# Line sweeps of a recurrent convolution: a group's four images interleaved position by position in the working line, PSUM and the sum, in place of image after image

## The chip, the cores and the metric

One core of a Trainium2 chip runs the whole program. The metric is device time in microseconds (us), the median over runs. Engines are named as in the profile: PE is TensorE's matmuls, PEld its weight loads, DVE is VectorE, ACT is ScalarE, POOL is GpSimd, SP is SyncE.

## What is computed

Eight images of 128 channels and 64 x 64 pixels pass through four layers, each of which adds its result to its input. The change touches layer 1 alone. There the image, after a group norm, is swept four times. Each step adds to a line of pixels the rectified convolution of the line before it, which has just been made:

```python
def _propagate(x, w, axis, reverse):
    xm = jnp.moveaxis(x, axis, 0)
    if reverse:
        xm = xm[::-1]
    def step(prev, cur):
        new = cur + jax.nn.relu(_conv1d(prev, w))
        return (new, new)
    _, outs = jax.lax.scan(step, xm[0], xm[1:])
...
x = _propagate(x, w_down, 2, False)
x = _propagate(x, w_up, 2, True)
x = _propagate(x, w_right, 3, False)
x = _propagate(x, w_left, 3, True)
```

`_conv1d` has 9 taps along the line and mixes all 128 channels. Sweeps 0 and 1 go over the rows of the image (down, then up), sweeps 2 and 3 over its columns (right, then left). Each has 63 steps, and no step can start before the one before it in the same image is done.

## The kernel before, in words

The function is `layer1`. Channels lie on the 128 partitions. All eight images stay in SBUF in one tile, `X`, as image, row, column; the sweeps work in place. The images form two groups (`NG` = 2) of four (`NI` = 4), and `s` is the group. The two groups take turns, so that TensorE convolves one while VectorE and ScalarE finish the other: 4 sweeps x 63 lines x 2 groups = 504 turns.

`line(d, s, t)` is the view of `X` that holds line t of sweep d for the four images of group s: in sweeps 0 and 1 four rows, so 64 neighbouring words an image; in sweeps 2 and 3 four columns, so 64 words an image that lie 64 words (256 bytes) apart.

TensorE multiplies in float32r, and fp32 accuracy comes from splitting both operands in a rounded part (hi) and a rest (lo). A turn of group s goes:

- ACT, `round_line` (line 225 of the file): hi = line, rounded. DVE, `rest_of_line` (line 290): lo = line - hi. Both write `prop_parts` (`parts[s]`), which holds hi and lo with a zero at either end of each line.
- PE, line 276: 9 matmuls, one a tap, of `w_lo` with hi, of 240 to 256 columns, into the half `ps[s][:, 1]` of the PSUM bank. Then line 281: 9 matmuls of `w_hi` with hi and lo together, of 480 to 512 columns, into both halves. Edge taps are cut to an even number of positions (`INSIDE`). Line 276 waits for hi (`s_hi`), line 281 for lo (`s_lo`), and the last matmul signals `s_conv`.
- DVE, three instructions: line 305 copies half 1 of the bank to `prop_sum`, line 307 adds half 0, and line 309 does line = max(sum, 0) + line in place in `X`. They are followed by the rest of the new line (290), which has to wait for ACT's rounding (225), which waits for 309.

The order is written out by hand, an instruction stream for each engine with semaphores between them; each engine does what it is given in order. On DVE it is 305, 307, 309, 290 of group 0, then of group 1, then the next line:

```python
with dve.Fori(1, H) as t:
    for s in range(NG):
        dve.wait_ge(s_conv[s], t + LINES * d)
        ...
        rest_of_line(d, t, s)
        if s == 0 and d == 3:
            add_first_x1(t - 1)
```

ACT has beside it, in sweep 0 only, the group norm of the next row (line 230). In sweep 3 DVE adds the layer's input to image 0 (line 296, every other turn). POOL makes `w_lo` once a sweep and prepares weights of layer 2. The other layers have their own functions and come before and after, with a barrier of all engines between.

Of the kernel before, what the change touches and what calls it, by code (L numbers as in the profile page):

```python
# [16 lines left out]
F32 = mybir.dt.float32  # L17
F32R = mybir.dt.float32r
U32 = mybir.dt.uint32
ALU = mybir.AluOpType  # L20
# [3 lines left out]
P = 128  # L24
B, H, W = 8, 64, 64
# [107 lines left out]
def layer1(nc, G, outer, x1_dram):  # L133
# [5 lines left out]
    NG, NI, PAD, LINES = 2, G.NI, 1, H - 1  # L139
    HALFWAY = H // 2  # L140
    MID = TAPS // 2
    INSIDE = [(k, max(0, MID - k) // 2 * 2, W - max(0, k - MID) // 2 * 2) for k in (MID, *range(MID), *range(MID + 1, TAPS))]
    with ExitStack() as ctx:
        def sb(name, shape, dt=F32):
            return ctx.enter_context(nc.sbuf_tensor(name, shape, dt))

        def sem(name):
            return ctx.enter_context(nc.semaphore(name))
        weights2 = Layer2Weights(nc, G, outer, ctx)
        raw = sb("prop_raw", [P, TAPS * P])  # L150
        w_hi = sb("prop_w_hi", [P, 2, TAPS * P], F32R)
        w_lo = sb("prop_w_lo", [P, 2, TAPS * P], F32R)
        parts = [sb(f"prop_parts{s}", [P, 2, NI, W + 2 * PAD], F32R) for s in range(NG)]
        hi = [t[:, 0, :, :] for t in parts]
        lo = [t[:, 1, :, :] for t in parts]
        zero = sb("prop_zero", [P, NI, PAD])
        ps = [ctx.enter_context(nc.psum_tensor(f"prop_ps{s}", [P, 2, NI, W], F32)) for s in range(NG)]
        sums = [sb("prop_sum", [P, NI, W])] * NG
        s_zero, s_edge = sem("p_zero"), sem("p_edges_zero")
        s_late = sem("p_second_halves_landed")  # L160
        s_norm = [sem(f"p_S_normed{s}") for s in range(NG)]
# [13 lines left out]
        def line(d, s, t):  # L175

            idx = t if d % 2 == 0 else t * -1 + (H - 1)
            if d < 2:
                return XV[:, NI * s:NI * s + NI, idx, :]
            return XV[:, NI * s:NI * s + NI, :, idx]  # L180

        with nc.Block() as block:
            @block.sync
            def _(sp):
                sp.dma_start(raw[:], G.d[names[0]]).then_inc(s_raw, 16)
                for b in range(NI, B):
                    sp.dma_start(G.X[:, b, 0:HALFWAY * W], x1_dram[:, b * HW:b * HW + HALFWAY * W]).then_inc(G.x_landed[b], 16)
                for b in range(G.KEEP, B):
                    sp.dma_start(G.X[:, b, HALFWAY * W:HW], x1_dram[:, b * HW + HALFWAY * W:(b + 1) * HW]).then_inc(s_late, 16)
                weights2.load(sp)  # L190
                sp.dma_start(first_x1[:].rearrange("p h w -> p (h w)"), x1_dram[:, 0:HW]).then_inc(G.first_x1_landed, 16)
                for d in range(1, 4):
                    sp.wait_ge(s_wlo, d)
                    sp.dma_start(raw[:], G.d[names[d]]).then_inc(s_raw, 16)
# [72 lines left out]
            @block.tensor  # L267
            def _(pe):
                pe.wait_ge(s_edge, 8)
                for d in range(4):  # L270
                    pe.wait_ge(s_wlo, d + 1)
                    with pe.Fori(1, H) as t:
                        for s in range(NG):
                            pe.wait_ge(s_hi[s], t + H * d)
                            for k, a, b in INSIDE:
                                pe.matmul(ps[s][:, 1, :, a:b], w_lo[:, d % 2, k * P:(k + 1) * P],  # L276
                                          hi[s][:, :, PAD + a + k - MID:PAD + b + k - MID],
                                          start=(k == MID), stop=False, skip_group_check=True)
                            pe.wait_ge(s_lo[s], t + H * d)
                            for k, a, b in INSIDE:  # L280
                                mm = pe.matmul(ps[s][:, :, :, a:b], w_hi[:, d % 2, k * P:(k + 1) * P],  # L281
                                               parts[s][:, :, :, PAD + a + k - MID:PAD + b + k - MID],
                                               start=False, stop=(k == TAPS - 1), skip_group_check=True)
                            mm.then_inc(s_conv[s], 1)

            @block.vector
            def _(dve):
                def rest_of_line(d, t, s):
                    dve.wait_ge(s_hi[s], t + (1 + H * d))
                    dve.tensor_tensor(lo[s][:, :, PAD:PAD + W], line(d, s, t), hi[s][:, :, PAD:PAD + W].bitcast(F32),  # L290
                                      ALU.subtract).then_inc(s_lo[s], 1)

                def add_first_x1(t):
                    dve.wait_ge(s_lo[0], t + (1 + H * 3))
                    x = line(3, 0, t)[:, 0, :]
                    dve.tensor_tensor(x, x, first_x1[:, :, t * -1 + (H - 1)], ALU.add).then_inc(s_added, 1)
                for d in range(4):
                    for s in range(NG):
                        rest_of_line(d, 0, s)
                    if d == 3:  # L300
                        dve.wait_ge(G.first_x1_landed, 16)
# [3 lines that stand above are left out]
                            dve.tensor_copy(sums[s][:], ps[s][:, 1, :, :]).then_inc(s_sum[s], 1)  # L305
                            dve.wait_ge(s_sum[s], 2 * t + (2 * LINES * d - 1))
                            dve.tensor_tensor(sums[s][:], ps[s][:, 0, :, :], sums[s][:], ALU.add).then_inc(s_sum[s], 1)
                            dve.wait_ge(s_sum[s], 2 * t + 2 * LINES * d)
                            dve.scalar_tensor_tensor(line(d, s, t), sums[s][:], 0.0, line(d, s, t), ALU.max,  # L309
                                                     ALU.add).then_inc(s_new[s], 1)  # L310
                            rest_of_line(d, t, s)
                            if s == 0 and d == 3:
                                add_first_x1(t - 1)
                for s in range(NG):
                    dve.wait_ge(s_lo[s], 4 * H)
                add_first_x1(H - 1)
                dve.wait_ge(s_added, H)
# [1534 lines left out]
```

## Time and profile before

| | us |
|---|---|
| median of 3 runs | 7821.44 |
| lowest and highest run | 7798.07, 7832.47 |
| the profiled execution | 7801.72 |
| its span, which the rows below divide | 7799.9 |

Busy over the whole span: PE 75%, DVE 68%, POOL 53%, ACT 46%, weight loads 43%. Layer 1's sweeps take from 2141 to 3774 us, a fifth of the span; layer 0 lies before them and layers 2 and 3 behind. The shares of the whole are averages over those layers and tell nothing of the sweeps, so the rows below are taken from inside each sweep.

### The profile page before, as it was taken

The numbers are of one execution on the slowest core, as the hardware profiler recorded it, in microseconds if no ns is written. First come the engines' busy times: TensorE is split into PE (matmuls) and PEld (weight loads), VectorE is DVE, ScalarE is ACT, GpSimd is POOL, SyncE is SP. The second block draws the span as 40 slices with busy tenths as digits, with TensorE's granted clock in tenths as the row PEclk, the third lists the DMA queues.
The fourth block names the chain that finished last, engine by engine and source line by source line (L and its number), as shares of the span: only waits on it lengthen the run. The fifth ranks groups of instructions, "written<-read, shape, count | busy, mean of one in ns | idle before, by whom it ended". The sixth has DMA issues, their size and how long they took to land. (4 is left out here: it accounts for less than half of the span.)

```text
span 7799.9 us, 91527 instructions
## 1 busy us (share of the span) xinstructions
PE 5869.8 (75%) x21659; PEld 3337.9 (43%) x21659; DVE 5308.8 (68%) x12779; ACT 3557.2 (46%) x7357; POOL 4119.9 (53%) x3880
## 2 busy tenths in 40 slices
PE   5999999999899999999865665656656565565432
PEld 2444444444388888888532322323222222232211
DVE  6999999999855556666465666556565665665557
ACT  4878888888755112222233333333333333333333
POOL 4999999999800001000055555556555555565663
PEclk9999999999999999999987777867778777787665
DMA  5544444444410001000166666566665666666667
GB/s 189 180 173 175 171 170 169 172 165 170 165 52 3 3 0 44 0 0 0 50 176 204 178 186 190 163 196 183 189 194 157 205 175 186 191 176 184 178 182 264
DMA packets 325623, 1132.63 MB, mean 145 GB/s; under 512 B 58859, under 2 KB 59901, under 8 KB 283300
## 3 DMA queue, kind: packets, MB, share of 16 engines
q0 software_dynamic: 188224, 629.56, 27.8%
q1 hardware_dynamic: 136948, 498.69, 17.9%
q14 instruction: 367, 3.01, 0.1%
q8 instruction: 84, 1.38, 0.1%
HBM read 997.72 MB, written 130.29 MB: 145 GB/s over the span
## 5 line engine op out<-in xcount | busy, mean ns | idle before, releaser
L1276 POOL DMA_INDIRECT d_ring<-corner_table,d_idx_now x2304 | 2218.9, 963 | 1704.5 <-issue 979.8
L1474 PE MATMUL d_ps_s<-small,d_mix 128*128 128x128 f32 x2304 | 478.7, 344 | 1317.3 <-DVE d_mix L1646 788.2
L980 POOL TENSOR_TENSOR X<-X 128x512 f32<-128x512 f32 x1024 | 1289.9, 1277 | 167.6 <-DVE X L1018 149.8
L1646 DVE SCALAR_TENSOR_TENSOR d_acc<-d_ring,d_w_now,d_mix 128x128 f32<-128x128 f32 x2304 | 661.0, 355 | 726.7 <-ACT d_mix L1322 347.1
L281 PE MATMUL prop_ps<-prop_parts,prop_w_hi 128*128 128x496 f32 (+2 forms) x4536 | 1142.1, 396 | 0.0
L1018 DVE TENSOR_TENSOR_SCAN X<-X,m_pB 128x512 f32<-128x512 f32 x896 | 1133.9, 1271 | 0.0
L874 PE MATMUL m_pY<-X,small 128*128 128x512 f32 x2048 | 1040.5, 605 | 90.8 <-POOL X L980 90.7
L1474 PEld LDWEIGHTS d_ps_s<-small,d_mix 128*128 128x128 f32 x2304 | 318.8, 172 | 1839.6 <-issue 981.1
L1322 ACT ACTIVATE d_mix<-d_ring,d_w_now 128x128 f32<-128x128 f32 x2304 | 732.5, 391 | 797.7 <-DMA d_ring<-corner_table,d_idx_now 724.0
L281 PEld LDWEIGHTS prop_ps<-prop_parts,prop_w_hi 128*128 128x128 f32 x4536 | 818.7, 189 | 162.1
L1406 PE MATMUL d_ps_out<-d_samp,d_dcn_w 128*128 128x512 f32 x1152 | 825.7, 809 | 46.3 <-ACT X L1309 34.0
L225 ACT ACTIVATE prop_parts<-X 128x256 fp32r (+1 forms) x512 | 276.6, 541 | 1178.1 <-DVE X L309 1177.6
L885 PE MATMUL m_pB<-m_bcs,m_pick 128*128 128x512 f32 x1027 | 759.6, 740 | 0.0
L1008 DVE TENSOR_TENSOR m_pB<-m_dtx,m_pB 128x512 f32<-128x512 f32 x1024 | 694.6, 679 | 92.4 <-PE m_pB L885 67.7
L941 ACT ACTIVATE X<-m_dtv,m_A 128x512 f32<-128x512 f32 x1027 | 688.5, 713 | 96.6 <-POOL m_dtv L737 75.0
L1646 DVE SCALAR_TENSOR_TENSOR d_mix<-d_ring,d_w_now,d_acc 128x128 f32<-128x128 f32 x2304 | 647.1, 341 | 86.6 <-remote 52.6
L1646 DVE SCALAR_TENSOR_TENSOR d_acc<-d_ring,d_w_now,d_acc 128x128 f32<-128x128 f32 x2304 | 649.6, 349 | 48.2 <-DVE d_acc L1646 21.5
L276 PE MATMUL prop_ps<-prop_parts,prop_w_lo 128*128 128x248 f32 (+2 forms) x4536 | 636.4, 285 | 20.9 <-ACT prop_parts L225 11.0
L276 PEld LDWEIGHTS prop_ps<-prop_parts,prop_w_lo 128*128 128x128 f32 x4536 | 608.3, 190 | 84.4 <-ACT prop_parts L225 40.1
L874 PEld LDWEIGHTS m_pY<-X,small 128*128 128x128 f32 x2048 | 363.3, 189 | 471.0 <-POOL X L980 281.3
L290 DVE TENSOR_TENSOR prop_parts<-X,prop_parts 128x256 fp32r<-128x256 f32 x512 | 267.5, 523 | 370.5 <-ACT prop_parts L225 370.3
L1371 ACT ACTIVATE d_tT<-l_ps_b 128x512 f32<-128x512 f32 x240 | 142.6, 594 | 709.4 <-remote 506.9
(232 smaller groups left out, 7840.5 us busy)
## 6 DMA issues: line engine op xcount, KB each, us to landing
X<-c_scratch SPq DMA_DIRECT2D x256, 1024.0 KB, 4.9
corner_table<-d_tT SPq DMA_DIRECT2D x248, 256.0 KB
d_ring<-corner_table,d_idx_now POOLq DMA_INDIRECT x2304
X<-in_x SPq DMA_DIRECT2D x8, 2048.0 KB, 15.2
m_res<-in_x SPq DMA_DIRECT2D x64, 256.0 KB, 4.5
x_scratch<-m_res SPq DMA_DIRECT2D x64, 256.0 KB, 2.1
x_scratch<-X SPq DMA_DIRECT2D x8, 2048.0 KB
b_x<-x_scratch POOLq DMA_DIRECT2D x16, 1024.0 KB, 11.7
```

The costliest lines, as they stand in the source:

```text
L276: pe.matmul(ps[s][:, 1, :, a:b], w_lo[:, d % 2, k * P:(k + 1) * P], hi[s][:, :, PAD + a + k - MID:PAD + b + k - MID], start=(k == MID), st ...
L281: mm = pe.matmul(ps[s][:, :, :, a:b], w_hi[:, d % 2, k * P:(k + 1) * P], parts[s][:, :, :, PAD + a + k - MID:PAD + b + k - MID], start=Fal ...
L874: pe.matmul(pY[:], G.ident, hc[:, n % NHC, :], start=False, stop=(n == NS - 1), skip_group_check=True).then_inc(s.sum, 1)
L885: pe.matmul(pB[:, n % NB, :], T.pick[:, n:n + 1].to_broadcast([P, P]), bcs[:, par, :], start=True, stop=True).then_inc(s.B, 1)
L980: pool.tensor_tensor(hc[:, n % NHC, :], h[:, n, :], Cb[:, n, :], ALU.mult).then_inc(s.HC, 1)
L1008: dve.tensor_tensor(pB[:, n % NB, :], dtx[:, c % 2, :], pB[:, n % NB, :], ALU.mult).then_inc(s.U, 1)
L1018: dve.tensor_tensor_scan(h[:, n, :], dA[:, n % NDA, :], pB[:, n % NB, :], T.zero[:, 0:1] if c == 0 else h[:, n, CH - 1:CH], ALU.mult, ALU. ...
L1276: pool.indirect_dma_start(out=ring[:, m % RING, :], out_offset=None, in_=flat, in_offset=bass.IndirectOffsetOnAxis(ap=idx_now[:, c % 2, m: ...
L1322: r0 = act.activation(R[:, k % 3, t, :], ring[:, m % RING, 0:P], ACT.Copy, scale=w_now[:, c % 2, 4 * m:4 * m + 1])
L1406: pe.matmul(ps_out[:], dcn_w[:, k, :], samp[:, k % 3, :], start=(k == 0), stop=(k == TAPS - 1)).then_inc(s_dcn, 1)
L1474: turned = pe.transpose(ps_s[k % 3][:, t, :], R[:, k % 3, t, :], G.ident)
L1646: mixed = dve.scalar_tensor_tensor(R[:, k % 3, t, :] if corner == 3 else acc[:, t, :], ring[:, m % RING, corner * P:(corner + 1) * P], w_n ...
```

## The change

The tiles `prop_parts`, `prop_ps` and `prop_sum` hold the same numbers in another order. They were (half,) image, position; now they are (half,) position, image, so that the four images' values of one position are neighbours. `X` keeps its order. The matmuls and the two DVE instructions that read PSUM go over the tiles in their order. ACT's rounding, DVE's rest and line 309, which also touch `X`, still go image by image, so in `prop_parts` and `prop_sum` they now step four words (16 bytes) from each element to the next.

```diff
@@ -150,12 +150,12 @@
-        parts = [sb(f"prop_parts{s}", [P, 2, NI, W + 2 * PAD], F32R) for s in range(NG)]
-        hi = [t[:, 0, :, :] for t in parts]
-        lo = [t[:, 1, :, :] for t in parts]
+        parts = [sb(f"prop_parts{s}", [P, 2, W + 2 * PAD, NI], F32R) for s in range(NG)]
+        hi = [t[:, 0, :, :].rearrange("p w i -> p i w") for t in parts]
+        lo = [t[:, 1, :, :].rearrange("p w i -> p i w") for t in parts]
         zero = sb("prop_zero", [P, NI, PAD])
-        ps = [ctx.enter_context(nc.psum_tensor(f"prop_ps{s}", [P, 2, NI, W], F32)) for s in range(NG)]
-        sums = [sb("prop_sum", [P, NI, W])] * NG
+        ps = [ctx.enter_context(nc.psum_tensor(f"prop_ps{s}", [P, 2, W, NI], F32)) for s in range(NG)]
+        sums = [sb("prop_sum", [P, W, NI])] * NG
@@ -273,13 +273,13 @@
                             for k, a, b in INSIDE:
-                                pe.matmul(ps[s][:, 1, :, a:b], w_lo[:, d % 2, k * P:(k + 1) * P],
-                                          hi[s][:, :, PAD + a + k - MID:PAD + b + k - MID],
+                                pe.matmul(ps[s][:, 1, a:b, :], w_lo[:, d % 2, k * P:(k + 1) * P],
+                                          parts[s][:, 0, PAD + a + k - MID:PAD + b + k - MID, :],
                                           start=(k == MID), stop=False, skip_group_check=True)
                             pe.wait_ge(s_lo[s], t + H * d)
                             for k, a, b in INSIDE:
-                                mm = pe.matmul(ps[s][:, :, :, a:b], w_hi[:, d % 2, k * P:(k + 1) * P],
-                                               parts[s][:, :, :, PAD + a + k - MID:PAD + b + k - MID],
+                                mm = pe.matmul(ps[s][:, :, a:b, :], w_hi[:, d % 2, k * P:(k + 1) * P],
+                                               parts[s][:, :, PAD + a + k - MID:PAD + b + k - MID, :],
                                                start=False, stop=(k == TAPS - 1), skip_group_check=True)
@@ -306,7 +306,7 @@
-                            dve.scalar_tensor_tensor(line(d, s, t), sums[s][:], 0.0, line(d, s, t), ALU.max,
+                            dve.scalar_tensor_tensor(line(d, s, t), sums[s][:].rearrange("p w i -> p i w"), 0.0, line(d, s, t), ALU.max,
                                                      ALU.add).then_inc(s_new[s], 1)
```

No instruction is added, dropped or moved on any engine; only the shapes on PE differ. On PE, the matmuls of one turn (the loop body of lines 276 and 281; the shape is that of the output):

```order
-L276 MATMUL prop_ps<-prop_parts,prop_w_lo 128x4x60
-L276 MATMUL prop_ps<-prop_parts,prop_w_lo 128x4x62 x2
+L276 MATMUL prop_ps<-prop_parts,prop_w_lo 128x240
+L276 MATMUL prop_ps<-prop_parts,prop_w_lo 128x248 x2
 L276 MATMUL prop_ps<-prop_parts,prop_w_lo 128x256 x2
```

The matmuls of line 281 change from 128x8x60 and 128x8x62 to 128x2x240 and 128x2x248. What was read as one run an image and half (4 runs, or 8) is now one run a half (1, or 2); this holds for the full-length taps as well, whose input had the two zeros between one image and the next.

## Rows read from the trace of the kernel before

**Rows 1.** Busy time by engine in each of the four sweeps, columns in the second line.
```profile
core 0: us, PE busy (x) PEld busy (x) DVE busy (x) ACT busy (x) POOL busy (x), PEclk, DMA share, GB/s
2141.40:2549.40 408.00, 404.90 (x2268) 352.37 (x2268) 214.39 (x502) 222.29 (x627) 2.67 (x1) 0.99 0.08 30
2549.40:2953.40 404.00, 401.88 (x2267) 350.62 (x2268) 214.87 (x506) 54.51 (x129) 2.64 (x1) 1.00 0.01 2
2953.40:3363.60 410.20, 404.38 (x2281) 351.22 (x2280) 280.66 (x512) 87.73 (x132) 33.84 (x53) 1.00 0.08 21
3363.60:3773.60 410.00, 406.77 (x2260) 337.74 (x2259) 279.27 (x567) 83.42 (x126) 0.00 (x0) 1.00 0.00 0
```

**Rows 2.** Timeline, one turn of sweep 1 (start us, us busy, engine).
```profile
2705.76 1.25 PE L276 MATMUL prop_ps<-prop_parts,prop_w_lo 128*128 128x256 f32 x9
2705.96 0.42 DVE L305 COPY prop_sum<-prop_ps 128x256 f32<-128x256 f32 x1 [0.66 <-PE prop_ps L281]
2706.42 0.42 DVE L307 TENSOR_TENSOR prop_sum<-prop_ps,prop_sum 128x256 f32<-128x256 f32 x1
...
2706.84 2.26 PE L281 MATMUL prop_ps<-prop_parts,prop_w_hi 128*128 128x512 f32 x9
2706.99 0.42 DVE L309 SCALAR_TENSOR_TENSOR X<-prop_sum,X 128x256 f32 x1
2707.53 0.42 ACT L225 ACTIVATE prop_parts<-X 128x256 fp32r x1 [2.69 <-DVE X L309]
2707.99 0.43 DVE L290 TENSOR_TENSOR prop_parts<-X,prop_parts 128x256 fp32r<-128x256 f32 x1 [0.57 <-ACT prop_parts L225]
...
2708.94 1.24 PE L276 MATMUL prop_ps<-prop_parts,prop_w_lo 128*128 128x256 f32 x9
```

**Rows 3.** Timeline, one turn of sweep 2.
```profile
3154.75 0.43 DVE L305 COPY prop_sum<-prop_ps 128x256 f32<-128x256 f32 x1
3155.21 0.42 DVE L307 TENSOR_TENSOR prop_sum<-prop_ps,prop_sum 128x256 f32<-128x256 f32 x1
...
3155.79 0.76 DVE L309 SCALAR_TENSOR_TENSOR X<-prop_sum,X 128x256 f32 x1
3156.67 0.67 ACT L225 ACTIVATE prop_parts<-X 128x256 fp32r x1 [2.55 <-DVE X L309]
3157.36 0.62 DVE L290 TENSOR_TENSOR prop_parts<-X,prop_parts 128x256 fp32r<-128x256 f32 x1 [0.82 <-ACT prop_parts L225]
...
3157.94 0.42 DVE L305 COPY prop_sum<-prop_ps 128x256 f32<-128x256 f32 x1
```

**Rows 4.** Groups in 2555 to 2950 us, sweep 1 (busy us, mean ns, idle before).
```profile
L290 DVE TENSOR_TENSOR prop_parts<-X,prop_parts 128x256 fp32r<-128x256 f32 x124 | 52.8, 426 | 73.2 <-ACT prop_parts L225 73.2
L305 DVE COPY prop_sum<-prop_ps 128x256 f32<-128x256 f32 x124 | 52.7, 425 | 89.7 <-PE prop_ps L281 89.7
L309 DVE SCALAR_TENSOR_TENSOR X<-prop_sum,X 128x256 f32 x124 | 52.7, 425 | 19.5 <-DVE prop_sum L307 10.7
L225 ACT ACTIVATE prop_parts<-X 128x256 fp32r x124 | 51.9, 418 | 344.6 <-DVE X L309 344.6
```

**Rows 5.** The same groups in 2955 to 3360 us, sweep 2.
```profile
L309 DVE SCALAR_TENSOR_TENSOR X<-prop_sum,X 128x256 f32 x127 | 96.6, 760 | 17.8
L290 DVE TENSOR_TENSOR prop_parts<-X,prop_parts 128x256 fp32r<-128x256 f32 x128 | 79.2, 619 | 103.1 <-ACT prop_parts L225 102.9
L305 DVE COPY prop_sum<-prop_ps 128x256 f32<-128x256 f32 x126 | 53.5, 424 | 2.0 <-PE prop_ps L281 2.0
L225 ACT ACTIVATE prop_parts<-X 128x256 fp32r x126 | 83.3, 661 | 319.0 <-DVE X L309 319.0
```

**Rows 6.** Line 96 before the sweeps: three short additions with gaps in every operand.
```profile
L96 DVE TENSOR_TENSOR sums<-sums x3: 189/194/225, 2129.9 to 2130.4; 128x64 f32<-128x64 f32 x1, 128x32 f32<-128x32 f32 x1, 128x16 f32<-128x16 f32 x1
```

## The prediction

> **What bounds the kernel now.** The change touches only the line sweeps, so I read those alone and look for what sets the length of one turn. The view of busy time by stretch comes first [rows 1]: the four sweeps take 408, 404, 410 and 410 us, 1632 in all, with the granted TensorE clock at 0.99 to 1.00, the 2.4 GHz level. With 126 turns a sweep (63 lines, 2 groups) a turn takes 3.2 to 3.25 us. PE is busy for 98 to 99% of every sweep, which makes it look like the bound of all four. That has to be tested against the other engines' order.
>
> The timeline of sweep 1 [rows 2] says yes for that sweep. PE starts line 276 at 2705.76 and again at 2708.94, a turn of 3.18 us. DVE waits for PE before its copy (0.66 us in this turn, 89.7 us in the 124 turns counted [rows 4]). PE bounds.
>
> The timeline of sweep 2 [rows 3] says no. The turn is the same, 3.19 us from copy to copy (3154.75 to 3157.94), but DVE no longer waits for PE: 2.0 us in 126 turns [rows 5]. Its four instructions and ACT's rounding between them form a closed loop, each step released by the one before:
> - copy to add 0.46 us, add to line 309 0.58, line 309 to ACT 0.88, ACT to rest 0.69, rest to the next copy 0.58: 3.19 us.
>
> So in sweeps 2 and 3 DVE and ACT bound the turn, with PE level with them. Sweep 3 has the same loop with line 296 beside it (410 us too). What differs from sweep 1 is only the reading and writing of columns of X. The same loop in sweep 1 [rows 2] is 0.46 + 0.57 + 0.54 + 0.46 up to the start of the rest, and 0.42 more until a copy could start (the rest's own 0.426 [rows 4]; in sweep 2 the copy follows the rest a little before its end): 2.45 us. It has 0.74 us of room under PE's 3.19.
>
> **What the change takes from PE.** It shortens no column count, it joins runs. The 9 matmuls of line 276 have 3 x 256 + 4 x 248 + 2 x 240 = 2240 columns, those of line 281 twice as many. At one column a cycle of 2.4 GHz that is 0.93 and 1.87 us. In the timeline [rows 2] the first nine take 1.08 us (2705.76 to 2706.84), the other nine 2.10 (to 2708.94). The excess is 0.15 and 0.23 us, or 16 ns for a matmul of 4 runs and 26 ns for one of 8. If that is a price by run, it is 2.5 ns a run over a fixed 6. With 1 and 2 runs the excess becomes 8.5 and 11 ns, 0.18 us a turn in place of 0.38. PE's turn falls from 3.18 to an estimated 2.98 us. The bounds: 3.18 (the excess goes with the columns, not the runs) and 2.80 (all of it goes). I take 2.98, because twice the runs over twice the columns would have doubled the fixed part as well.
>
> **What it adds to DVE and ACT.** Three instructions now step four words in a tile where they ran through neighbours. The price of a step is in the trace only for columns of X, by sweep 2 against sweep 1 [rows 4, 5], the same instructions with the same 256 elements:
> - line 290, one stepping input: 426 to 619 ns, +0.19 us.
> - line 309, one stepping input and a stepping output: 425 to 760, +0.335. The second stream adds 0.14 to what the first costs.
> - line 225 on ACT, a stepping input: 418 to 661, +0.24.
>
> Those steps are 256 bytes, the new ones 16. The nearest row to that is line 96 [rows 6]: its 64-element form, in groups of four neighbours, takes 225 ns, the 32-element form in pairs 194, the 16-element form with single words 32 bytes apart 189. From 64 to 32 elements 31 ns go, about 1 ns an element; from 32 to 16 only 5, where 16 would be due. So short steps of single words cost too, by some 11 ns on 16 elements, 0.7 ns each, in an instruction with three such streams. On 256 elements that is 0.18. I take the column prices for the first and second stream, since these are the same instructions on the same tiles.
>
> Sweeps 0 and 1, where X is read and written in runs:
> - line 309, one stepping input: +0.19 (bounds 0 and 0.335).
> - line 225, a stepping output: no row has it; between 0.14 (a second stream on DVE) and 0.24 (an input on ACT): +0.19, bounds 0 and 0.335.
> - line 290, a stepping input and a stepping output: +0.335 (bounds 0 and 0.47, which is 0.335 and one more stream).
> - The loop becomes 2.45 + 0.715 = 3.165 us against PE's 2.98: DVE and ACT take over as the bound, and the turn goes from 3.19 to 3.165. 252 turns x -0.025 = **-6 us**. What PE gains is not used here.
>
> Sweeps 2 and 3, where these instructions step already and the loop has no room:
> - line 309 gets its third stream: between 0 and 0.14, +0.10.
> - line 290 gets a second and a third: between 0 and 0.28, +0.20.
> - line 225 gets a stepping output beside the stepping input: between 0 (the two overlap) and 0.24, +0.12.
> - +0.42 us on a loop that is wholly on the path: 252 x 0.42 = **+106 us**. PE's gain is worth nothing here, since PE only stays level today.
>
> The copy and the add (305, 307) keep one run of 256. The eight small writes of the zeros stay as they are, and the starts of the four sweeps, each one pass through the chain of steps, add under 1 us each. In sweep 0 ACT does the next row's norm too (222 us busy in 408 [rows 1]); 0.19 us more a turn leaves it idle for over 1 us a turn. The clock should hold: PE would be busy for some 83% of the turn, and no sweep shows it at another level. Layers 0, 2 and 3 keep their work, so what the sweeps lose is lost whole.
>
> The sum is +100 us: 7802 for the profiled execution becomes 7902. The median of the runs lies 20 us above that execution, so for the median I give **7920 us**, +1.3%.
>
> A rule weighed against this: sweep 2's row for one stepping input is 619 - 426 = 193 ns on 256 elements, 0.75 ns each, and for two streams 1.3 ns each [rows 4, 5]. The Trainium skill (Vector Engine (DVE) Microarchitecture Reference, Measured stream behaviour on trn2) has 1.05 ns an element in runs of at least two words, 1.73 for one source that hops each element, and 1.98 with all three operands hopping: the later streams nearly free. By it line 290 and line 309 would lose only 0.06 us each in sweeps 2 and 3, and the sum would be about +20 us. The trace agrees on the first stream and not on the second; the second rival below is this case, from rows. The same section has 2.5 ns for steps of 24 words, which is the fourth.
>
> **The rivals.**
> 1. The forecast: steps of four words cost about what columns do. Chance **0.45**. Its own range is 7860 to 8000.
> 2. Penalties saturate: the first stepping stream costs 0.19, later ones on the same instruction nothing. For it: each stream may hide behind another's stall. Against: line 309's second stream cost 0.14. Sweeps 0 and 1: 2.45 + 0.19 + 0.19 + 0.14 = 2.97, so PE at 2.98 bounds, -0.20 x 252 = -50. Sweeps 2 and 3: only ACT, +0.12, 252 x 0.12 = +30. Together -20: 7801 for the median. **0.20**, within 0.5%.
> 3. The other side, faster: a step of four words is free and only long steps cost. Then the loop stays at 2.45 us in sweeps 0 and 1, PE's 2.98 decides, and -0.20 x 252 = -50 us; in sweeps 2 and 3 the loop of 3.19 still binds, 0. That is 7771. It decides where the three steps together add under 0.1 us in sweeps 2 and 3 and under 0.5 in sweeps 0 and 1. For it: the steps are a sixteenth of a column's. Against: line 96's short steps cost. **0.13**. The gain cannot be much larger, for half the turns do not wait for PE. The Trainium skill (SBUF — State Buffer, Door 1, the note on cachelines) says that one can stride for free over 4 fp32, and that each access which crosses to a new 16-byte line pays; a step of exactly 16 bytes stands between the two halves of that sentence. No row of this trace has that step.
> 4. Short steps cost more than columns: each instruction pays what line 309's two streams do (0.335), and line 290 0.47. Sweeps 0 and 1: 2.45 + 1.14 = 3.59, +0.40 x 252 = +101. Sweeps 2 and 3: the same 1.14 on top, +287. Together up to 8210; the near end is 8080. **0.09**.
> 5. The change does nothing for PE: the excess goes with the columns. Then sweeps 0 and 1 stay at 3.19, since 3.165 is still under it, and the sum is +106: 7927. It is told from the forecast only on PE's rows. **0.13**.
>
> **How the numbers follow.** Less than about 0.5% (39 us) can't be told from no change here. Faster by more is rival 3, 0.13. Within it is rival 2, 0.20. Slower is the forecast, rivals 4 and 5, 0.67. The range reaches from 7780, which leaves out half of rival 3, to 8090, which leaves out most of rival 4; about 0.14 is outside.
>
> **What would show it.** Right: in sweeps 0 and 1 line 309 near 0.62 us, line 290 near 0.76, line 225 near 0.61; DVE's idle time before line 305 gone there; nine matmuls of line 276 in about 1.01 us and of line 281 in 1.97 when nothing makes them wait, and PE waiting for ACT's rounding in every sweep. In sweeps 2 and 3 line 309 near 0.86, 290 near 0.82, 225 near 0.78, and turns of 3.6 us. The two row sweeps would keep their 404 to 408 us, the two column sweeps would take some 460 each. Wrong: durations of 0.42 us at these lines in sweep 1 (rival 3), or column sweeps that stay near 410 us (rival 2 or 3), or row sweeps above 440 us (rival 4).

## The result, and the profile after

The change made the kernel a little faster, where I had forecast it 1.3% slower.

| | before | after |
|---|---|---|
| first comparison, median us (range) | 7807.15 (7781.91 to 7832.47) | 7746.90 (7727.66 to 7764.90) |
| ratio, 95% interval | | 0.9927 (0.990 to 0.9954) |
| second comparison, another chip (e5) | 6979.42 | 6954.26 |
| ratio | | 0.9966 (0.9954 to 0.9978) |
| third comparison, a third chip (e10) | 7804.80 | 7763.12 |
| ratio | | 0.9943 (0.992 to 0.9966) |

The first and third chip need 830 us more than the second for the same program. Layers 2 and 3 account for it: 4026 us in the profile of before, 3193 to 3195 in the profiles of e5 and e2, whose layers 2 and 3 are the same. So the sweeps are best compared by themselves. Busy time by engine in each sweep of the changed kernel (the columns are named in the first line):

```profile
core 0: us, PE busy (x) PEld busy (x) DVE busy (x) ACT busy (x) POOL busy (x), PEclk, DMA share, GB/s
2141.80:2539.20 397.40, 390.28 (x2268) 346.18 (x2268) 262.89 (x505) 234.61 (x629) 2.68 (x1) 0.99 0.08 31
2539.20:2930.00 390.80, 387.84 (x2269) 344.73 (x2270) 258.47 (x508) 85.16 (x129) 2.66 (x1) 1.00 0.01 2
2930.00:3331.30 401.30, 397.66 (x2269) 333.92 (x2269) 273.02 (x508) 87.27 (x129) 36.16 (x53) 1.00 0.08 22
3331.30:3747.60 416.30, 411.43 (x2268) 335.15 (x2268) 283.57 (x569) 85.38 (x127) 0.00 (x0) 1.00 0.00 0
```

Against [rows 1] the sweeps take 1606 us in place of 1632, 27 less. Measured from the first matmul of one sweep to that of the next, the four went from 402, 405, 405 and 412 us to 389, 391, 401 and 416 (with 8 us ahead of the first for its weights). The row sweeps gain 13 and 14 us; the column sweeps stay, one 4 us shorter and one 4 longer.

Groups of the changed kernel in 2555 to 2900 us, sweep 1 (busy us, mean ns, idle before); the first four are VectorE's and the last ScalarE's:

```profile
L290 DVE TENSOR_TENSOR prop_parts<-X,prop_parts 128x256 fp32r<-128x256 f32 x113 | 71.3, 631 | 93.9 <-ACT prop_parts L225 93.9
L309 DVE SCALAR_TENSOR_TENSOR X<-prop_sum,X 128x256 f32 x112 | 68.7, 613 | 17.6 <-DVE prop_sum L307 9.6
L305 DVE COPY prop_sum<-prop_ps 128x256 f32<-128x256 f32 x113 | 48.0, 425 | 0.0
L307 DVE TENSOR_TENSOR prop_sum<-prop_ps,prop_sum 128x256 f32<-128x256 f32 x113 | 47.9, 424 | 3.9
L225 ACT ACTIVATE prop_parts<-X 128x256 fp32r x113 | 74.5, 659 | 271.6 <-DVE X L309 271.6
```

The same in 2950 to 3310 us, sweep 2:

```profile
L309 DVE SCALAR_TENSOR_TENSOR X<-prop_sum,X 128x256 f32 x114 | 87.0, 763 | 16.0
L290 DVE TENSOR_TENSOR prop_parts<-X,prop_parts 128x256 fp32r<-128x256 f32 x114 | 72.6, 637 | 94.5 <-ACT prop_parts L225 94.5
...
L225 ACT ACTIVATE prop_parts<-X 128x256 fp32r x114 | 76.7, 673 | 283.0 <-DVE X L309 283.0
```

Read beside [rows 4] and [rows 5]: where nothing stepped before, each of the three instructions now costs 0.19 to 0.24 us more (309: 425 to 613 ns, 290: 426 to 631, 225: 418 to 659). Where one operand or more stepped already, the new steps cost 0.003, 0.018 and 0.012 us. VectorE's wait for PE before line 305 in sweep 1 is gone (89.7 us in [rows 4], 0.0 now), so its loop has grown to nearly the length of TensorE's turn.

The timeline of one turn of sweep 1 after the change:

```profile
2602.05 1.19 PE L276 MATMUL prop_ps<-prop_parts,prop_w_lo 128*128 128x256 f32 x9
2602.25 0.42 DVE L305 COPY prop_sum<-prop_ps 128x256 f32<-128x256 f32 x1
2602.71 0.42 DVE L307 TENSOR_TENSOR prop_sum<-prop_ps,prop_sum 128x256 f32<-128x256 f32 x1
...
2603.07 2.19 PE L281 MATMUL prop_ps<-prop_parts,prop_w_hi 128*128 128x512 f32 x9
2603.27 0.61 DVE L309 SCALAR_TENSOR_TENSOR X<-prop_sum,X 128x256 f32 x1
2604.01 0.67 ACT L225 ACTIVATE prop_parts<-X 128x256 fp32r x1 [2.36 <-DVE X L309]
2604.71 0.63 DVE L290 TENSOR_TENSOR prop_parts<-X,prop_parts 128x256 fp32r<-128x256 f32 x1 [0.83 <-ACT prop_parts L225]
...
2605.10 1.20 PE L276 MATMUL prop_ps<-prop_parts,prop_w_lo 128*128 128x256 f32 x9
```

The turn is 3.05 us here from one start of line 276 to the next. As a mean over the middle of sweep 1 it is 3.06, against 3.18 before. (A sweep's length over its 126 turns is more, 3.10 against 3.21, for it holds the sweep's start.) The nine matmuls of line 276 take 1.02 us in place of 1.08, those of line 281 2.03 in place of 2.10; as means of the sweep they lose 0.05 and 0.06 us.

Which of the two bounds a turn shows in how long after TensorE's last matmul the copy of line 305 starts. In the row sweeps it is 0.04 us in nearly every turn, before the change and after it: TensorE bounds. In sweep 2 the matmuls before the copy at 3157.94 of [rows 3] were these:

```profile
3155.64 2.26 PE L281 MATMUL prop_ps<-prop_parts,prop_w_hi 128*128 128x512 f32 x9
```

and in the changed kernel, in the same sweep:

```profile
3101.65 2.19 PE L281 MATMUL prop_ps<-prop_parts,prop_w_hi 128*128 128x512 f32 x9
...
3103.67 0.63 DVE L290 TENSOR_TENSOR prop_parts<-X,prop_parts 128x256 fp32r<-128x256 f32 x1 [0.83 <-ACT prop_parts L225]
...
3104.22 0.42 DVE L305 COPY prop_sum<-prop_ps 128x256 f32<-128x256 f32 x1
```

Before the change TensorE ended at 3157.90 and the copy followed 0.04 us later, as in 117 of the 126 turns of that sweep. After it TensorE ends at 3103.84 and the copy starts 0.38 us later. So TensorE still bounded sweep 2 before the change, and the loop of VectorE and ScalarE bounds it now; the mean turn went from 3.18 to 3.15 us. In sweep 3 the copy came 0.41 us after TensorE already before the change: the loop bounds it in both kernels, with turns of 3.235 and 3.267 us. The 0.032 us more match the three new steps (0.003 + 0.018 + 0.012).

### The profile page after: what moved, and what is told of

It reads as the page before. It is cut to its first block and busy times, and to the rows that moved or that the text cites. A ratio compares the mean times of both kernels' runs of the same rounds, so it can differ in the third digit from the quotient of the medians.

```text
span 7725.9 us, 91527 instructions
## 1 busy us (share of the span) xinstructions
PE 5818.9 (75%) x21659; PEld 3292.0 (43%) x21659; DVE 5401.5 (70%) x12779; ACT 3601.9 (47%) x7357; POOL 4123.7 (53%) x3880
## 5 line engine op out<-in xcount | busy, mean ns | idle before, releaser
L281 PE MATMUL prop_ps<-prop_parts,prop_w_hi 128*128 128x496 f32 (+2 forms) x4536 | 1108.3, 388 | 0.0
L225 ACT ACTIVATE prop_parts<-X 128x256 fp32r (+1 forms) x512 | 340.5, 666 | 1106.8 <-DVE X L309 1105.9
L276 PEld LDWEIGHTS prop_ps<-prop_parts,prop_w_lo 128*128 128x128 f32 x4536 | 581.4, 189 | 113.6 <-ACT prop_parts L225 87.4
L290 DVE TENSOR_TENSOR prop_parts<-X,prop_parts 128x256 fp32r<-128x256 f32 x512 | 324.5, 634 | 434.0 <-ACT prop_parts L225 434.0
```

Source lines behind the costliest of these rows:

```text
L276: pe.matmul(ps[s][:, 1, a:b, :], w_lo[:, d % 2, k * P:(k + 1) * P], parts[s][:, 0, PAD + a + k - MID:PAD + b + k - MID, :], start=(k == MI ...
L281: mm = pe.matmul(ps[s][:, :, a:b, :], w_hi[:, d % 2, k * P:(k + 1) * P], parts[s][:, :, PAD + a + k - MID:PAD + b + k - MID, :], start=Fal ...
```

## The experiments

### e1: single instructions, each form by itself

Behind the last layer of the kernel before, one block with each form in a loop; the rest of the program is as before. Below, `four` is a tile of 256 words read or written with a step of four, `run` one without a step, `col` a column of `X`, four images.

```diff
+                for _r in range(8):
+                    dve.tensor_tensor(four(2), run(0), four(1), ALU.add).then_inc(s_op, 1)
...
+                for _r in range(24):
+                    last = pe.matmul(q_ps[:, 0:512].rearrange("p (n l) -> p n l", n=8), w32[:], rows(m32, 8, 2), start=True, stop=True, skip_group_check=True)
```

> The kernel before, with a block of single instructions behind its last layer, each form repeated 8 times (VectorE, ScalarE) or 24 times (TensorE). VectorE, 256 fp32 elements, 0.43 us with no stepping operand. Theory A (a step costs once: what counts is whether any operand steps from element to element, not how many): one, two or three stepping operands of four words all take 0.61 to 0.64 us, a column of X as input the same, and only reading and writing the same column in place takes 0.76. Theory B (each stream adds its price): two stepping operands 0.76 or more wherever they lie, three 0.85 or more. ScalarE: 0.42 without, 0.66 with a step on either side, and on both 0.67 (A) or 0.9 (B). TensorE, 512 float32r columns back to back: theory R (a price by run): 1 run 219 ns start to start, 2 runs 221, 8 runs 231 to 240, 32 runs over 270; theory C (a price by column): 231 to 240 in all of them.

Single instructions on VectorE (min/median/max ns). The nine, from the top: no step; one input `four`; output `four`; input and output `four`; all three `four`; one input a column; a column read and written; the same with a `four` input as well (line 309 in the column sweeps); one input with a step of two words.

```profile
L1928 DVE TENSOR_TENSOR X<-X x8: 425/426/426, 6968.3 to 6971.5; 128x256 f32<-128x256 f32 x8
L1932 DVE TENSOR_TENSOR X<-X x8: 604/605/607, 6971.9 to 6976.4; 128x256 f32<-128x256 f32 x8
L1940 DVE TENSOR_TENSOR X<-X x8: 609/610/610, 6982.2 to 6986.7; 128x256 f32<-128x256 f32 x8
L1944 DVE TENSOR_TENSOR X<-X x8: 616/618/623, 6987.4 to 6991.9; 128x256 f32<-128x256 f32 x8
L1948 DVE TENSOR_TENSOR X<-X x8: 608/609/615, 6992.6 to 6997.1; 128x256 f32<-128x256 f32 x8
L1952 DVE TENSOR_TENSOR X<-X x8: 583/586/590, 6997.7 to 7002.1; 128x256 f32<-128x256 f32 x8
L1968 DVE TENSOR_TENSOR X<-X x8: 699/699/700, 7018.8 to 7023.9; 128x256 f32<-128x256 f32 x8
L2000 DVE SCALAR_TENSOR_TENSOR X<-X x8: 719/722/723, 7060.5 to 7065.8; 128x256 f32<-128x256 f32 x8
L2004 DVE TENSOR_TENSOR X<-X x8: 425/426/427, 7066.6 to 7069.8; 128x256 f32<-128x256 f32 x8
```

ScalarE: no step; input `four`; output `four`; a column as input and a `four` output; an input with a step of two words.

```profile
L1844 ACT ACTIVATE X<-X x8: 416/416/417, 7116.8 to 7119.9; 128x256 f32<-128x256 f32 x8
L1848 ACT ACTIVATE X<-X x8: 652/653/654, 7120.4 to 7125.2; 128x256 f32<-128x256 f32 x8
L1852 ACT ACTIVATE X<-X x8: 651/652/652, 7125.9 to 7130.6; 128x256 f32<-128x256 f32 x8
L1864 ACT ACTIVATE X<-X x8: 656/657/657, 7141.9 to 7146.7; 128x256 f32<-128x256 f32 x8
L1868 ACT ACTIVATE X<-X x8: 428/428/428, 7147.4 to 7150.6; 128x256 f32<-128x256 f32 x8
```

Theory A holds for steps of four words. One such stream costs 0.18 us on VectorE and 0.24 on ScalarE, and two or three cost no more than one (0.61 to 0.62 us in all on VectorE, 0.66 on ScalarE). Theory B is right only for a column read and a column written in one instruction: 0.70. It does not take the same column: with one column read and another written it was 0.70 too. In the sweeps line 309 took 0.76 where its form here takes 0.70 to 0.72; why is not shown. On VectorE two words cost nothing, three words 0.07 us (494 ns, line 2008), four words the whole price.

TensorE, 24 matmuls of 512 float32r columns each, in 8, 32 and 64 runs:

```profile
L1896 PE MATMUL q_ps<-q_m,q_w x24: 395/395/400, 7199.5 to 7204.8; 128*128 128x512 f32 x24
L1900 PE MATMUL q_ps<-q_m,q_w x24: 419/420/420, 7210.9 to 7216.8; 128*128 128x512 f32 x24
L1902 PE MATMUL q_ps<-q_m,q_w x24: 447/447/450, 7217.0 to 7223.5; 128*128 128x512 f32 x24
```

Neither R nor C. As a mean from one start to the next it is 234 ns in 8 runs, 257 in 32 and 282 in 64 (a row's duration is 161 to 165 more, for a matmul overlaps the next); 1, 2 and 4 runs are at 233 to 234 as well. At 256 columns it was 114 for 1 run, 120 for 4 and 124 for 8. So breaks cost, but at 512 columns 8 runs took no more than one. Only the input is broken in these rows, the output is one run. The same 512 columns in bf16 took 216 ns, in 1 run or in 32.

### e2 and e3: the copy on ScalarE, before and after the change

Line 305 moves from VectorE to ScalarE, in both kernels alike, which should make the loop of VectorE and ScalarE 0.46 us shorter, so that TensorE's own turn shows in every sweep.

```diff
+                def copy_half(d, t, s):
+                    act.wait_ge(s_conv[s], t + LINES * d)
+                    act.activation(sums[s][:], ps[s][:, 1, :, :], ACT.Copy).then_inc(s_sum[s], 1)
...
-                            dve.wait_ge(s_conv[s], t + LINES * d)
-                            dve.tensor_copy(sums[s][:], ps[s][:, 1, :, :]).then_inc(s_sum[s], 1)
```

> The kernel before with the copy of line 305 moved from VectorE to ScalarE. The loop of VectorE and ScalarE falls by 0.46 us a turn, so TensorE bounds all four sweeps. If TensorE's turn is 3.19 us in the old order of the images: the sweeps take 402, 402, 404 and 404 us, the layer some 1622 us against 1632 (total -10 us, no difference that can be measured). If what follows layer 1 takes longer or shorter by tens of us in a profile although nothing in it has changed, that is scatter of those layers.

> The changed kernel with the same copy on ScalarE. TensorE alone bounds: the turn shows its price in the new order. With the 3.05 us seen in the sweeps of the changed kernel: every sweep 385 to 389 us, the layer some 1555 us, -50 us against the changed kernel and -78 against the one before (total 7720 to 7740 if the later layers stay at 4026 us, 7680 if they stay at the 3978 of the changed kernel's profile). If the loop were still the bound (rival), 390, 391, 401, 416 as in the changed kernel.

e2: 6964.65 us against 6971.89, ratio 0.9993 (0.9984 to 1.0002). Its sweeps take 402, 405, 404 and 406 us. e3: 6917.07 us, ratio 0.9922 (0.9908 to 0.9936). Its sweeps:

```profile
2140.50:2539.00 398.50, 391.22 (x2269) 346.92 (x2269) 211.09 (x379) 298.24 (x755) 2.67 (x1) 0.99 0.08 31
2539.00:2929.60 390.60, 387.77 (x2268) 344.34 (x2268) 210.22 (x381) 133.24 (x255) 2.64 (x1) 1.00 0.01 2
2929.60:3320.50 390.90, 387.70 (x2268) 344.57 (x2268) 231.57 (x381) 135.75 (x256) 35.58 (x53) 1.00 0.08 22
3320.50:3711.60 391.10, 387.82 (x2268) 344.44 (x2268) 243.52 (x444) 134.18 (x254) 0.00 (x0) 0.99 0.00 0
```

The four (the first less its 8 us) lie within 4 us of each other in e2 and within 1 in e3, so TensorE alone bounds there. As means over the middle of a sweep its turn is 3.18 us in the old order and 3.06 in the new, so the new order saves 0.12 us a turn, 14 us a sweep, where TensorE bounds. e3's sweeps came out at 390 to 391 us where I had expected 385 to 389, and the layer at 1571 us for 1555, since 3.05 us a turn leaves out the start of each sweep. In the changed kernel the row sweeps were at that bound already; e3 brings the column sweeps down to it, 10 and 25 us. e3 beats both kernels.

e2 says something on the kernel before as well. With a shorter loop sweep 2 still took 404 us (405 before), and only sweep 3 gained, 412 to 406. So TensorE, and not the loop, bounded sweep 2 in the kernel before.

### e5 and e10: the changed kernel on other chips

> The changed kernel itself, again. In the first comparison it was 60 us faster, of which the sweeps show 27 (1632 to 1606 us), the rest lies in layers 2 and 3, whose code is the same. Theory S (that rest is scatter of those layers): the sweeps take 389, 391, 401 and 416 us again and the total falls by 27 us, 0.4%. Theory K (it belongs to the change): the total falls by 55 to 60 us again.

> The changed kernel a third time. On the chip of the first comparison the kernel before takes 7800 us and scatters by 0.4%, on that of the second 6979 us and by 0.1%; layers 2 and 3 make the difference. On a chip of the slow kind: theory S (scatter): total lower by 27 us within an interval of some 20 us, theory K (the later layers gain another 30 us there): lower by 55 to 60 us. On one of the fast kind: 25 to 27 us again. The sweeps take 389, 391, 401 and 416 us on either.

e5: -25 us (0.9966, which reaches from 15 to 32 us), sweeps 389, 391, 401, 417. That fits the layer's own 27 us. e10: -42 us (0.9943, which reaches from 27 to 62 us), sweeps 389, 391, 402, 418. In the profiles on slow chips layers 2 and 3 took 4026 us before the change (the one profile that there is), and 3978 (the first comparison) and 4003 us (e10) after it; with the same code there e9, below, took 4032. On the fast chip theory S holds. On the slow chips the total fell by more than the sweeps explain in both comparisons, and the first interval, from 36 to 78 us, leaves the 27 out; that of e10 just holds them. That some of it belongs to the change on such chips is not excluded.

### e11: e3 again, on a slow chip

> The changed kernel with line 305 on ScalarE, again beside the changed kernel itself on one chip: 390 or 391 us for each sweep, 35 us under the changed kernel in the layer and 61 under the kernel before; total 55 to 61 us under the kernel before on a fast chip, the same give or take 20 on a slow one.

7737.94 us, ratio 0.9914 (0.9885 to 0.9943), -67 us. Sweeps 389, 391, 391, 391; layer 1 takes 1570 us, 38 under the changed kernel beside it. Here the sweeps' gain of 62 us and the total's agree, and layers 2 and 3 took 4019 us. So a larger gain in layer 1 did not come with a shorter time in the layers behind it.

### e6: two images side by side

The line and PSUM hold the images in two pairs, so that ScalarE and VectorE step two words; the sum stays image by image.

```diff
-        parts = [sb(f"prop_parts{s}", [P, 2, W + 2 * PAD, NI], F32R) for s in range(NG)]
+        parts = [sb(f"prop_parts{s}", [P, 2, 2, W + 2 * PAD, 2], F32R) for s in range(NG)]
...
-                            dve.tensor_copy(sums[s][:], ps[s][:, 1, :, :]).then_inc(s_sum[s], 1)
+                            dve.tensor_copy(sums[s][:].rearrange("p (g j) w -> p g j w", j=2), ps[s][:, 1, :, :, :].rearrange("p g w j -> p g j w")).then_inc(s_sum[s], 1)
```

> Two images side by side in place of four: in the line ACT and DVE step two words, TensorE reads 2 and 4 runs in place of 1 and 2. The sum is kept image by image, so lines 305 and 307 read PSUM with a step of two words and line 309 steps nowhere but in columns. A step of two words is free (the probe had 0.426 us for it on VectorE, 0.428 on ScalarE), so in sweeps 0 and 1 lines 309, 290 and 225 are back at 0.42 to 0.43 us if PSUM's step is free as well, and TensorE alone bounds there: if its gain needs the long runs, 395 to 400 us a sweep, if breaking the image-by-image order is enough, 390. Sweeps 2 and 3 stay at 400 to 405 and 412 to 416 us, bound by the loop. Sum 1605 to 1625 us for the layer.

6957.99 us, ratio 0.9969 (0.9957 to 0.9981); the layer 1611 us, the sweeps 392, 395, 401 and 415. VectorE in sweep 1 (2555 to 2900 us):

```profile
L290 DVE TENSOR_TENSOR prop_parts<-X,prop_parts 128x256 fp32r<-128x256 f32 x111 | 47.6, 429 | 67.6 <-ACT prop_parts L225 67.6
L305 DVE COPY prop_sum<-prop_ps 128x256 f32<-128x256 f32 x111 | 47.1, 425 | 67.3 <-PE prop_ps L281 67.3
L309 DVE SCALAR_TENSOR_TENSOR X<-prop_sum,X 128x256 f32 x111 | 47.1, 425 | 17.5 <-DVE prop_sum L307 9.6
```

All steps are free or nearly so (line 225 takes 438 ns there, against 418), and VectorE waits for PE again (67.3 us). TensorE keeps 60 to 70% of its gain with runs half as long: the sweep is 395 us, between 405 and 391, the mean turn 3.11, between 3.18 and 3.06. The column sweeps stay where the changed kernel had them, for their columns of X still set the loop.

### e7: the sum image by image

Lines 305 and 307 read PSUM with the step of four words, and line 309 has none.

```diff
-                            dve.tensor_copy(sums[s][:], ps[s][:, 1, :, :]).then_inc(s_sum[s], 1)
+                            dve.tensor_copy(sums[s][:], ps[s][:, 1, :, :].rearrange("p w i -> p i w")).then_inc(s_sum[s], 1)
```

> The changed kernel with the sum kept image by image: the step of four words moves from line 309 (SBUF) to lines 305 and 307 (PSUM). If VectorE reads PSUM with a step for nothing: 305 and 307 stay at 0.42 us, 309 falls from 0.61 to 0.42 in sweeps 0 and 1 and from 0.76 to 0.74 in sweeps 2 and 3. The loop in sweeps 0 and 1 falls from 3.06 to 2.87 us, and since TensorE's own turn is 3.08 there, nothing is gained: 389 and 391 us, and 399 and 413 behind. If instead the loop bounds sweeps 0 and 1 in the changed kernel: below 385 us. If PSUM's step costs 0.18 us each: the loop is longer by 0.17 us, 408 us in sweeps 0 and 1.

6952.98 us, ratio 0.9961 (0.9948 to 0.9975). In sweep 1:

```profile
L309 DVE SCALAR_TENSOR_TENSOR X<-prop_sum,X 128x256 f32 x113 | 48.1, 426 | 17.8 <-DVE prop_sum L307 9.8
...
L305 DVE COPY prop_sum<-prop_ps 128x256 f32<-128x256 f32 x112 | 47.5, 424 | 14.9 <-PE prop_ps L281 7.3
```

VectorE reads PSUM with a step for nothing, and line 309 is back at 426 ns. The loop is 0.19 us shorter, yet the row sweeps take 389 and 391 us as in the changed kernel. So TensorE bounds them in the changed kernel too, with the loop just under it (0.46 + 0.56 + 0.74 + 0.70 + 0.59 = 3.05 us in the timeline above). The column sweeps took 403 and 416 us, where I had expected 399 and 413.

### e8: TensorE's turn by itself, and beside the others

Behind the last layer, the 18 matmuls of a turn over and over, in either order, in five phases.

```diff
+                for _r in range(8):
+                    for k, a, b in TAPSET:
+                        last = pe.matmul(pb[:, 1, a:b, :], wq[:, k * P:(k + 1) * P], qb[:, 0, a + k - 3:b + k - 3, :], start=(k == 4), stop=False, skip_group_check=True)
...
```

> The kernel before, with a block behind its last layer that runs the 18 matmuls of a turn over and over, in the old and in the new order, first with every other engine idle, then beside VectorE in runs, VectorE with steps of four words, ScalarE with steps, and VectorE reading PSUM. A turn without a wait: theory R (what the new order saves is a price of run breaks in TensorE itself): 3.18 us old and 3.07 new with the others idle, no more beside them. Theory T (it is contention with VectorE and ScalarE for SBUF, which many short runs feel more): old and new alike, about 3.0, when idle, and apart only beside the others.

Eight turns with all other engines idle, first in the old order (by image), then in the new (by place):

```profile
L1853 PE MATMUL q_psa<-q_by_image,q_w x72: 273/282/292, 7049.1 to 7072.2; 128*128 128x248 f32 x32, 128*128 128x256 f32 x24, 128*128 128x240 f32 x16
L1855 PE MATMUL q_psa<-q_by_image,q_w x72: 382/394/407, 7050.2 to 7074.2; 128*128 128x496 f32 x32, 128*128 128x512 f32 x24, 128*128 128x480 f32 x16
L1858 PE MATMUL q_psb<-q_by_place,q_w x72: 274/278/284, 7074.4 to 7097.0; 128*128 128x248 f32 x32, 128*128 128x256 f32 x24, 128*128 128x240 f32 x16
L1860 PE MATMUL q_psb<-q_by_place,q_w x72: 374/387/403, 7075.5 to 7098.9; 128*128 128x496 f32 x32, 128*128 128x512 f32 x24, 128*128 128x480 f32 x16
```

Eight old turns take 7049.1 to 7074.4, 3.16 us each. Eight new ones take 7074.4 to 7099.1 (the last start and its 0.22 us), 3.09 each. Beside VectorE in runs, VectorE stepping, ScalarE stepping and VectorE reading PSUM, the turns were the same to 2 ns. Theory T, contention, falls: TensorE by itself is 0.07 us a turn faster in the new order. That is not the whole 0.12 of the sweeps, where the old turn is 0.02 us longer than here and the new one 0.02 shorter. Where the rest comes from is open; the probe writes one PSUM tile over and over, the sweeps take turns between two.

Nor is it shown which breaks cost. In e1, with only the input broken, 8 runs of 512 columns took no more than one; here the nine matmuls of 480 to 512 columns gain 0.045 us, and in the sweeps 0.06, over half of the whole gain. A kernel with the line interleaved and PSUM left image by image (e4) was to part reading from writing, and gave no result. The same program measured VectorE's reads of PSUM with a step of four words at 424 ns, as without.

### e9: a longer loop

Lines 305 and 307 write `prop_sum` image by image while they go over PSUM place by place; TensorE's work is unchanged.

```diff
-                            dve.tensor_copy(sums[s][:], ps[s][:, 1, :, :]).then_inc(s_sum[s], 1)
+                            dve.tensor_copy(sums[s][:].rearrange("p i w -> p w i"), ps[s][:, 1, :, :]).then_inc(s_sum[s], 1)
```

> The changed kernel with the sum kept image by image and lines 305 and 307 going over PSUM in its order, so that both write prop_sum (and 307 reads it) with a step of 64 words from each element to the next. TensorE's work is that of the changed kernel. By the probe 305 takes 0.60 us (+0.18), 307 with two such streams 0.70 (+0.28), and 309 is back without its step in sweeps 0 and 1 (-0.19). If VectorE's and ScalarE's loop sets the turn wherever it is longer than TensorE's 3.09: a turn of 3.33 us in sweeps 0 and 1, 420 us each in place of 389 and 391, and +0.45 us in sweeps 2 and 3, 456 and 473 us in place of 401 and 416; the layer 1780 us, the total +145 us against the kernel before, +2.1%. If some of it hides elsewhere (the loop not closed as I read it), less than half of that.

7902.97 us, ratio 1.0129 (1.0084 to 1.0174), +105 us, which is what the sweeps lost (1737 us, against 1632). Line 305 took 617 ns and line 307 619, not 700: its two streams count once again. The rows of the four sweeps:

```profile
2140.50:2553.90 413.40, 405.82 (x2268) 337.16 (x2268) 279.58 (x505) 234.63 (x629) 2.68 (x1) 0.99 0.07 30
2553.90:2964.30 410.40, 406.84 (x2269) 335.11 (x2269) 278.34 (x507) 84.89 (x129) 2.63 (x1) 1.00 0.00 1
2964.30:3413.80 449.50, 421.04 (x2269) 335.29 (x2269) 320.59 (x508) 86.39 (x129) 34.29 (x53) 1.00 0.07 19
3413.80:3877.70 463.90, 421.31 (x2268) 335.16 (x2268) 332.13 (x570) 84.30 (x127) 0.00 (x0) 0.99 0.00 0
```

With the durations measured in sweep 2 (305: 415 to 614 ns, 307: 424 to 618, 309: 763 to 752), the loop should be 0.38 us longer in the column sweeps, 48 us a sweep. Both became 48 us longer (401 to 450, 416 to 464). So the loop sets their turn in the changed kernel. My forecasts of 456 and 473, and of 420 in the row sweeps (405 and 410 measured, without the 8 us ahead of the first), were too high mainly because I had given line 307 two prices.

## Why the prediction was wrong, step by step

**What bounds the sweeps** was read rightly for three of the four. The row sweeps follow TensorE (e2, e7), and sweep 3 follows the loop of VectorE and ScalarE. In sweep 2 TensorE was the bound and not the loop: the copy started 0.04 us after the last matmul, and e2 with its shorter loop hardly gained there (405 to 404 us). I had read "2.0 us in 126 turns" of idle time before the copy as no wait. But the copy can start before the rest (290) is recorded as ended, by 0.04 us in [rows 3] and by 0.08 where no matmul holds it back (3104.30 and 3104.22 in the rows above), so a wait of that size counts as no idle time. The loop of 3.19 us that I added up held some 0.05 us of it and was 3.13 by itself, an estimate from these rows. So "PE's gain is worth nothing here" was off too: in sweep 2 it was worth the 4 us that the loop left.

**The price of the first stepping stream** was right: line 309 +0.19 forecast and +0.19 measured, line 225 +0.19 forecast and +0.24 measured. Rival 3, free steps, is out. So are rival 4, for the row sweeps did not lengthen, and rival 5, for TensorE's turn did shorten.

**The step that failed is the price of later streams.** "Line 309 gets its third stream: between 0 and 0.14, +0.10", line 290 "a second and a third ... +0.20", line 225 "+0.12" made 0.42 us a turn, +106 us. They measured 0.003, 0.018 and 0.012, together 0.033. That is the +4 us of sweep 3; in sweep 2 the loop stayed under TensorE's old turn even with them, and the sweep fell by 4 us. I had taken the 0.14 us between line 290 and line 309 in the column sweeps for the price of any second stream. In the probe only a column of X read and a column of X written in one instruction cost more than one stream (0.70 us). With a column and four words it is 0.62, with three times four words 0.61, and e9's line 307, which reads and writes `prop_sum` in steps of 64 words, took 0.62. The same error is in the row sweeps: line 290 +0.335 forecast, +0.205 measured, so the loop came to 3.05 us and not 3.165.

The Trainium skill (Vector Engine (DVE) Microarchitecture Reference, Measured stream behaviour on trn2), which I had weighed against my reading of the trace, was the better guide. Its 1.73 ns an element for one source hopping by 4 KiB, against 1.05 without, makes an estimate of 174 ns on 256 elements; 179 were measured for a step of four words (605 - 426). Its 1.98 with all three operands hopping is 0.93 over the 1.05; three streams of four words took 0.71 more an element than none (609 - 426, over 256), so here the later streams cost even less.

**TensorE's gain** was mis-sized. "2.5 ns a run over a fixed 6" gave 0.20 us a turn, 7.5 ns for a matmul of line 276 and 15 for one of line 281. In the sweeps it measured 0.12 us, 6 and 7 ns, and 0.07 alone (e8). Most of the error is in line 281: at 512 columns most of the excess stays with long runs as well. One run of 512 columns takes 233 ns in e1, 20 more than the 213 of the prediction's count of one column a cycle, where the prediction kept 11 for two runs.

**The sum by the measured terms**: the row sweeps -0.11 x 252 = -27 us, sweep 2 -4, sweep 3 +4, the whole -27. That is rival 2, "penalties saturate", by its mechanism. Its time was 7801 us, -20, and so near is half luck: it had a larger gain on PE (-50) and a loss on ScalarE (+30) that was not there. The first comparison's -60 us lies beyond it and beyond rival 3's -50, but the second's -25 us is what the sweeps give.

**What stays open** is, beside 0.04 us of TensorE's gain a turn and which breaks cost, the rest of the first comparison's gain: 60 us on one slow chip and 42 on another, of which the sweeps explain 27. e5 shows none of it on a fast chip, and e9 and e11 none on slow chips. The two profiled executions of the changed kernel on slow chips differ by 24 us in these layers, which is of the size in question. I hold scatter for likelier, and it isn't shown.

## What to carry to other kernels

Price a stepping operand by instruction, not by stream: one step of four words or more cost 0.16 to 0.19 us per 256 elements on VectorE and 0.21 to 0.24 on ScalarE, and more of them on the same instruction almost nothing, but for a column of X read and one written together (some 0.28 in place of 0.18). So put new steps where an instruction steps already, or into reads of PSUM. Before taking a difference between two rows as the price of one thing, ask what else differs between them; a probe of 8 repeats would have told. Test a bound by shortening the other chain: a loop that adds up to the turn can hold a short wait. And when two bounds lie within a few per cent of each other, a gain on one is worth only what the other leaves; here moving one 0.4 us copy to ScalarE, which had room, was worth 8 us of the sweeps without the change (e2) and 35 us on top of it (e3).

## What was not expected of the hardware

- A step of two words is free on VectorE (426 ns, as without) and nearly so on ScalarE (428 ns, against 416). On VectorE three words cost over a third of the price (494 ns), four words the whole (604).
- VectorE reads PSUM with a step of four words as fast as without (424 ns).
- A float32r matmul of 512 columns in one run takes 233 ns from start to start at the 2.4 GHz level, more than twice the 114 of 256 columns, and the same 512 in bf16 216. Breaks in the input's runs cost float32r time and bf16 none (float32r, 256 columns: 114, 120 and 124 ns for 1, 4 and 8 runs; 512 columns: 233 and 257 for 1 and 32; bf16, 512 columns: 216 in 1 and in 32).
- The same program took 830 us more on some chips than on others, 12% of the whole, all of it in layers 2 and 3 (4026 us against 3195), and the sweeps of the changed kernel differed by less than 3 us. What in those layers differs is not shown.
